# A norm weight of 1024 columns multiplied into gelu rows by GpSimd, in place of scaling 128x114 blocks as they leave PSUM, with all engine orders of the later stages written anew

## What is computed

```
h = h + _L1_ffn_ref(_layernorm(h))        # LN: D = 256
# _L1_ffn_ref:
h = einsum('btd,hd->bth', x, absmean(W_fc))      # 256 -> 1024, weights in {-1, 0, 1}
h = gelu(h, approximate=False)
h = (h - mu) * rsqrt(var + eps) * ln_w + ln_b    # over the 1024 columns
return einsum('bth,dh->btd', h, absmean(W_proj)) # 1024 -> 256
```

## Time and profile before

| | |
|---|---|
| three runs | 544.4, 544.42, 547.71 us; median 544.42 |
| the profiled execution | 544.11 us |
| its span from first to last record | 542.3 us |
| around the span | 1.8 us |
| PE / DVE / ACT / POOL busy | 92% / 70% / 52% / 36% of the span |
| bytes from HBM | 27.98 MB, the DMA engines nearly idle after 240 us |

### The profile page before, as it was taken

One profiled execution on the slowest core, in us unless ns is written; L12 is line 12 of the kernel. 1 busy time (PEld: TensorE's weight loads), 2 busy tenths in 40 slices (PEclk: granted clock), 3 DMA queues, 4 the chain that ended last, 5 costly groups with the idle time before them and its releaser, 6 DMA issues. The chain is left out here.

```text
span 542.3 us, 11847 instructions
## 1 busy us (share of the span) xinstructions
PE 498.7 (92%) x3814; PEld 418.8 (77%) x3814; DVE 380.1 (70%) x1009; ACT 280.1 (52%) x684; POOL 194.8 (36%) x257
## 2 busy tenths in 40 slices
PE   8989999999998888689999999999999998989994
PEld 8778877877786666468778888888888886877874
DVE  5554366466456767547898878778788787799884
ACT  4220321322223334547667776776776787665751
POOL 4232123132133311365464553543643601243311
PEclk9998999999999999999999999999999999999997
DMA  8934342432504100000000000000000000000000
GB/s 302 391 110 164 116 149 90 153 131 81 176 27 158 25 2 1 1 0 2 1 1 1 2 0 0 0 0 0 0 0 0 2 2 0 2 10 26 19 25 16
DMA packets 10992, 29.64 MB, mean 55 GB/s; under 512 B 2192, under 2 KB 3408, under 8 KB 10704
## 3 DMA queue, kind: packets, MB, share of 16 engines
q1 hardware_dynamic: 10960, 29.23, 16.0%
HBM read 27.98 MB, written 1.25 MB: 54 GB/s over the span
## 5 line engine op out<-in xcount | busy, mean ns | idle before, releaser
L378 POOL TENSOR_TENSOR h<-h,scaled 114x256 f32 (+1 forms) x88 | 68.5, 779 | 43.2 <-ACT scaled L695 36.5
L330 POOL TENSOR_TENSOR small<-small,half 114x1 f32<-114x1 f32 x44 | 28.6, 650 | 135.8 <-DVE small L966 135.8
L561 ACT ACTIVATE p_exp<-sc,cst 114x608 f32<-114x608 f32 x66 | 48.1, 794 | 26.8 <-DVE sc L1047 26.8
L2010 PE MATMUL bz<-ebuf 128*128 128x256 f32 x256 | 59.0, 383 | 0.0
L569 ACT ACTIVATE pt<-tb 114x456 f32<-114x456 f32 x66 | 34.4, 556 | 35.4 <-PE tb L1978 35.3
L2010 PEld LDWEIGHTS bz<-ebuf 128*128 128x128 f32 x256 | 47.9, 192 | 5.9
L1978 PE MATMUL tb<-cst,p_exp 114*114 114x114 f32 x352 | 44.1, 266 | 6.2 <-ACT pt L569 3.7
L2156 PE MATMUL score<-v,pt 114*114 114x137 f32 x352 | 48.5, 282 | 0.0
L695 ACT ACTIVATE scaled<-bank,gl 114x256 f32<-114x256 f32 x88 | 38.8, 471 | 18.1 <-PE bank L1897 10.3
L1978 PEld LDWEIGHTS tb<-cst,p_exp 114*114 114x114 f32 x352 | 35.2, 134 | 15.4 <-ACT pt L569 7.0
L2156 PEld LDWEIGHTS score<-v,pt 114*114 114x114 f32 x352 | 43.9, 178 | 1.8
(11 more groups left out here) (210 smaller groups left out, 1315.6 us busy)
## 6 DMA issues: line engine op xcount, KB each, us to landing
ebuf<-in_w_in SPq DMA_DIRECT2D x16, 512.0 KB, 4.3
ebuf<-in_w_out SPq DMA_DIRECT2D x16, 512.0 KB, 5.1
x_raw<-in_x_tiles SPq DMA_DIRECT2D x11, 342.0 KB, 3.1
out<-h SPq DMA_DIRECT2D x10, 114.0 KB
raw<-in_w_a SPq DMA_DIRECT2D x4, 256.0 KB, 4.2
ebuf<-in_fc SPq DMA_DIRECT2D x1, 1024.0 KB, 4.9
ebuf<-in_proj SPq DMA_DIRECT2D x1, 1024.0 KB, 7.0
raw<-in_w_a SPq DMA_DIRECT2D x2, 384.0 KB, 5.4
```

The lines of the kernel that those rows point to most:

```text
L378: gp.tensor_tensor(h[0:R, t, :], h[0:R, t, :], scaled[0:R, e % 4, :], ALU.add).then_inc(moe_acc, 1)
L561: act.activation(p_exp[0:R, :, b * S:(b + 1) * S], sc[0:R], ACT.Exp, bias=cst[0:R, CB + b:CB + b + 1], scale=SCALE).then_inc(exps, 1)
L2010: last = pe.matmul(bz[:, m * D:(m + 1) * D], ebuf[:, 0, c * D + m * P:c * D + (m + 1) * P], ebuf[:, 1, c * D:(c + 1) * D], start=(c == 0 a ...
```

## The change

1. `gel` becomes two buffers by tile parity; a third, `gel_w`, holds the weighted row. All lie in `ebuf`, which the expert and ternary weights have left by then; a row copy of the weight (`lnw_row`) is loaded there by one more DMA, once all four ternary steps are done.
2. POOL gets `d2_weigh`: per tile two multiplies of 114x512, after each half of gelu. `d2_turn` transposes `gel_w` and waits for each half by itself.
3. `d2_hi` and `d2_lo` no longer scale. Each evicts a half in one instruction of 128x456, in place of four of 128x114.
4. `d1_gelu(t)` now waits for the weighting and the statistics of tile t-2, no longer for the turns and statistics of t-1.
5. All order lists after the first loop, and the body of `c_step`, are different on PE, DVE, ACT and POOL. Apart from the ternary block the same instructions are in them.

```diff
-        gel = ebuf[:, 0, 0:HID]
+        gel = [ebuf[:, 0, 0:HID], ebuf[:, 1, HID:2 * HID]]
+        gel_w = ebuf[:, 0, HID:2 * HID]
+        lnw_row = ebuf[:, 1, 0:HID]
...
+            sp.wait_ge(tern, 8)
+            sp.dma_start(lnw_row[0:R], lnw).then_inc(row_w_in, 16)
...
+            def d2_weigh(t, halves):
+                if zero(t):
+                    gp.wait_ge(row_w_in, 16)
+                for q in halves:
+                    gp.wait_ge(gelu, 2 * t + q + 1)
+                    if q == 0:
+                        since(gp, gT_mm, 2 * t)
+                    cols = slice(q * 512, (q + 1) * 512)
+                    gp.tensor_tensor(gel_w[0:R, cols], gel[t % 2][0:R, cols], lnw_row[0:R, cols], ALU.mult).then_inc(weighted, 1)
...
                     if q == 0:
-                        since(act, gT_mm, 2 * t)
-                        since(act, g_stat, 4 * t - 2)
-                    act.activation(gel[0:R, q * 512:(q + 1) * 512], bk[1 + q][0:R, :], ACT.Gelu).then_inc(gelu, 1)
+                        since(act, weighted, 2 * t - 2)
+                        since(act, g_stat, 4 * t - 6)
+                    act.activation(gel[t % 2][0:R, q * 512:(q + 1) * 512], bk[1 + q][0:R, :], ACT.Gelu).then_inc(gelu, 1)
...
-                    for c in range(4):
-                        k = 4 * q + c
-                        last = act.activation(gth[:, k, :], score[:, q, c * R:(c + 1) * R], ACT.Copy, scale=lnwc[:, k:k + 1])
-                    last.then_inc(gT_hi, 1)
+                    act.activation(gth[:, 4 * q:4 * q + 4, :], score[:, q, 0:4 * R].rearrange("p (c r) -> p c r", c=4),
+                                   ACT.Copy).then_inc(gT_hi, 1)
...
-                    for c in range(4):
-                        k = 4 * q + c
-                        last = V.scalar_tensor_tensor(gtl[:, k, :], score[:, q, c * R:(c + 1) * R], lnwc[:, k:k + 1],
-                                                      gth[:, k, :].bitcast(F32), ALU.mult, ALU.subtract)
-                    last.then_inc(gT_lo, 1)
+                    V.tensor_tensor(gtl[:, 4 * q:4 * q + 4, :], score[:, q, 0:4 * R].rearrange("p (c r) -> p c r", c=4),
+                                    gth[:, 4 * q:4 * q + 4, :].bitcast(F32), ALU.subtract).then_inc(gT_lo, 1)
...
             def d2_turn(t, halves=(0, 1)):
-                pe.wait_ge(gelu, 2 * t + 2)
                 since(pe, gT_lo, 2 * t)
                 for q in halves:
+                    pe.wait_ge(weighted, 2 * t + q + 1)
...
-                        last = pe.transpose(score[:, q, c * R:(c + 1) * R], gel[0:R, k * P:(k + 1) * P], cst[0:R, CI:CI + R])
+                        last = pe.transpose(score[:, q, c * R:(c + 1) * R], gel_w[0:R, k * P:(k + 1) * P], cst[0:R, CI:CI + R])
...
             d1_fc(1, (0, 1))
+            d1_x(2)
             c3_r1(8)
+            d1_fc(2, (0,))
             c2_turn_p(10, (0,))
```

More of the change, by code:

```diff
@@ L798, in _ @@
             c1_gate(2)
             softmax_exp(0 + T, (0, 1, 2))
-            c1_scale(2, (0, 1, 2, 3))
-            c2_pt(0, (0, 1, 2))
+            c1_scale(2, (0, 1))
+            c2_pt(0, (0,))
+            c1_scale(2, (2,))
+            c2_pt(0, (1,))
+            c1_scale(2, (3,))
+            c2_pt(0, (2,))
             c1_scale(2, (4,))
             c2_pt(0, (3,))
+            c2_x(1, (0, 1))
+            c2_hi(1)
             c1_x(3)
-            c1_scale(2, (5,))
             c2_pv(0, (0, 1))
-            c2_x(1, (0, 1))
@@ new lines, in _ @@
+            c2_pv(0, (4, 5))
+            c2_mix(0)
+            softmax_exp(1 + T, (0, 1, 2))
+            c1_gate(3)
+            c2_pt(1, (0, 1, 2, 3))
+            c2_pv(1, (0,))
+            c3_att(0)
+            c2_pv(1, (1,))
+            c1_scale(3, (0, 1, 2))
+            c2_x(2, (0, 1))
+            c2_hi(2)
+            c1_scale(3, (3, 4))
+            c2_pv(1, (2, 3))
+            c2_rows(2)
+            c2_pv(1, (4, 5))
+            c2_q(2, (0,))
+            c3_x(0, (0, 1))
+            c2_q(2, (1,))
@@ L849, in _ @@
+            c2_pt(2, (2, 3))
             with act.Fori(5, T) as i:
@@ L870, in _ @@
             c1_scale(10, (7,))
[L871 removed]
+            c3_x(7, (0, 1))
+            c3_xhi(7)
+            softmax_exp(9 + T, (0, 1, 2))
             c3_rows(7)
[L873 to L877 removed]
+            c2_pt(9, (0, 1, 2, 3))
+            c3_relu(7, (0, 1, 2, 3))
             c2_x(10, (0, 1))
@@ L1578, in _ @@
+            gate(2, 2)
+            c2_aggr(1)
+            gate(2, 3)
+            c2_eps(1, (0,))
+            gate(2, 4)
+            aggr(n1, 4)
+            gate(2, 5)
+            c2_eps(1, (1,))
+            gate(2, 6)
+            gate(2, 7)
+            gate(2, 8)
+            c2_v(0, (0, 1))
+            normed2(1)
+            normed1(1)
+            ternary(0)
+            plus_eps(n1, 4)
+            c2_x(1)
+            ternary(1)
             c1_normed(4)
-            tern_th(1)
@@ L1580, in _ @@
-            normed2(1)
-            ternary(0)
-            ternary(1)
             c1_x(3)
-            normed1(1)
-            c2_x(1)
+            c2_k(1, (0, 1))
+            mix(0, 0)
             gate(3, 0)
             gate(3, 1)
+            mix(0, 1)
             gate(3, 2)
-            mix(0, 0)
-            mix(0, 1)
+            mix(0, 2)
+            c2_stats(2)
+            mix(0, 3)
+            softmax_max(1 + T)
+            mix(0, 4)
+            softmax_sub(1 + T, (0, 1))
+            mix(0, 5)
@@ L1613, in _ @@
             mix(0, 10)
+            gate(3, 6)
+            mix(0, 11)
+            mix(0, 12)
             normed2(2)
-            mix(0, 11)
+            gate(3, 7)
             normed1(2)
-            mix(0, 12)
-            ternary(2)
-            c1_x(4)
+            gate(3, 8)
             c3_sum(0)
-            c2_x(2)
             c3_stats(0)
@@ L1624, in _ @@
             plus_eps(n4, 0)
-            ternary(3)
+            c2_x(2)
+            ternary(2)
             c3_normed(0)
@@ L1660, in _ @@
             gate(10, 5)
+            d0_stats(0)
+            gate(10, 6)
+            aggr(nD, 0)
+            plus_eps(nD, 0)
+            gate(10, 7)
+            c2_x(9)
+            gate(10, 8)
             normed1(9)
-            gate(10, 6)
-            gate(10, 7)
-            gate(10, 8)
-            c2_x(9)
+            d1_norm(0)
+            d0_stats(1)
             c3_sum(7)
+            aggr(nD, 1)
             c3_stats(7)
             aggr(n4, 7)
-            d0_stats(0)
+            plus_eps(nD, 1)
@@ L1689, in _ @@
+            mix(8, 2)
+            d0_stats(2)
+            mix(8, 3)
+            aggr(nD, 2)
+            c3_normed(7)
+            mix(8, 4)
+            d1_x(0)
+            plus_eps(nD, 2)
+            softmax_max(9 + T)
+            mix(8, 5)
+            softmax_sub(9 + T, (0, 1))
+            mix(8, 6)
+            c2_v(9, (0,))
+            c3_x(7)
+            mix(8, 7)
             c2_stats(10)
-            plus_eps(nD, 1)
             c2_aggr(10)
-            mix(8, 5)
-            c2_eps(10, (0, 1))
@@ L2295, in _ @@
             a2_pv(8)
-            a1_x(10)
+            a1_qk(10)
+            c1_x(0)
             scores(9, True)
             a2_wo(8)
-            a1_qk(10)
-            c1_x(0)
             a1_v(10)
+            c1_gate(0)
             a1_turn(9, (0, 1, 2, 3))
```

983 lines of the change are left out of this document (474 added, 509 removed).

## The result

The changed kernel takes 556.4 us (median of 4 executions, 553.8 to 559.6) where the kernel before takes 544.4: a ratio of 1.022, 95% interval 1.019 to 1.025. The forecast was 547.8 us with a range up to 552.5, so the time lies above it. The profiled execution of after is the slowest of the four: 559.6 us, span 557.8, mean granted clock 0.966 (the other three 0.972 to 0.981; before 0.988 in the profiled one).

What follows compares the result with a forecast made beforehand. PE was taken as fully busy in the second loop, with time to win only in its idle time between the loops and waits in the ternary block. Sum: 544.1 - 2.5 + 2.4 + 5.8 + 1.0 - 3.0 = 547.8 us, range 540.5 to 552.5.

Steps and rivals of the forecast that it cites:

- Between the loops: Stretch between the two hardware loops: new order and less slow clock together save 2.5 us, bounds -5 and +2.
- the order: Between the loops: the new order fills PE's waits for the quotient in two first-attention tiles, -1.4 us.
- -1.1 for about two thirds of the slow stretch at 241.73: Between the loops: about two thirds of before's slow-clock stretch near 241.73 us goes, saving 1.1 us.
- The second loop: Six loop passes: c2_x waits through c2_pt on c1_gate, 0.4 us a pass, +2.4 us, bounds 0 and +6.
- The test named: Second loop: passes of 21.3 to 21.5 us, with PE idle ahead of c2_x, released by ACT, would show it right.
- The last softmax: Tile 10's exponentials: three table loads and gelus make PE wait at d1_fc(2), +5.8 us, bounds 0 and 7.
- the clock behind it: Products behind the last softmax's pause: PE's clock may fall, +1.0 us, bounds 0 to 1.6.
- The block: Ternary block: cheaper evictions leave six waits, 6.4 of 8.0 us, and no slow clock; -3.0 us, bounds +1 and -9.
- The first two: Rivals: softmax pause under 1 us and block gives 7, 537 us, chance 0.12; pause absent, block gives 3, 541, 0.15.
- the fifth: Rival, last softmax: table switches hold ACT 2.6 us for 1.28, 4 us more, 551.8 us; chance 0.04.
- A slower loop: Third rival, second loop: it costs 1 us per pass, 551.4 us; chance 0.12.
- That GpSimd sets the pace: Fourth rival, ternary block: multiply and turns form a ring, 5.2 us per tile against PE's 4.7, 553 us; chance 0.09.

Runs made afterwards that it cites:

- a_warm: Kernel before with the changed orders between the loops, plus useless PE products (fillers) in PE's waits there: 544.55 us, ratio 0.999.
- after_both: Changed kernel with fillers in PE's waits between the loops, and tile 1's gelu and d1_fc(2) moved later around the last softmax: 542.6 us, ratio 0.999.
- after_fix: Changed kernel with only tile 1's gelu and d1_fc(2) moved later around the last softmax, no fillers: 550.7 us.
- best_warm: after_both with the second loop's body put back to that of the kernel before: 540.8 us, ratio 0.992.
- best_plain: best_warm without the fillers in PE's waits between the loops: 545.7 us, ratio 1.001.
- b_gate: b_only with one swap on ACT: the gate's exponential behind the last eviction of transposed probabilities, not ahead: 545.5 us, ratio 1.002.
- b_only: Kernel before with the changed kernel's second-loop body on all four engines, all else as before: 548.9 us, ratio 1.010.
- b_two: b_only with two loop steps back at before's place, the Wf product on PE and the second relu pieces on ACT: 550.6 us.
- c_fix: Changed kernel with before's orders between the loops and loop body, and tile 1's gelu and d1_fc(2) moved later around the last softmax: 540.95 us, ratio 0.995.
- region C: The part of the change behind the second loop, with its functions; run alone, with the rest as in the kernel before: 547.6 us, ratio 1.008.
- c_nw3: c_noweight with three gelu buffers in place of two: 539.3 us.
- c_noweight: c_fix with GpSimd's 22 multiplies and the weight row's load left out, so the output lacks the norm weight: 549.6 us.

## Why the prediction was wrong, step by step

**Between the loops (forecast -2.5, bounds -5 and +2): this step failed.** Its first half, the order, was right in direction and too large: with full clock the new order stands 2.0 to 2.1 us ahead at the end of the second loop, and with the 1.6 us that the forecast itself gave to the slow stretch of before, that leaves some 0.4 to 0.5 us for the order (an estimate), where the term had 1.4. Its second half was "-1.1 for about two thirds of the slow stretch at 241.73", and this half has the wrong sign. I took the slow stretch of before as something that the new order could only shorten. It grew: after's profiled execution has a clock of 0.82 from 182 to 250 us, and the term came out at +6.3 at the product of tile 0, and at +7.3 with the 1.0 us of the next pass. A mean of 0.82 over 68 us is about 24 us at the lower level, and 0.97 is about 4; 20 us more at half speed cost up to 10 us (an estimate), and the runs at 0.82 stand 9.1 to 9.3 us behind those at 1.00. The rows of before held the warning, since waits stand close together there and the clock fell behind several of them, but none of my rivals had a longer slow stretch. The runs show the clock as the cause and not the waits themselves: the waits sum to the same 12.5 to 12.8 us, and work without use in them makes the kernel 6.6 (a_warm), 8.1 (after_both against after_fix) and 4.9 us (best_warm against best_plain) faster.

In after the clock is at its lower level soon after `c1_gate(0)` has waited 1.56 us at 205.56, and again behind the wait of 3.11 us ahead of the turns of tile 10:

```profile
208.00:212.00 4.00, 3.18 (x18) 2.15 (x20) 1.73 (x7) 0.99 (x3) 0.00 (x0) 0.50 0.00 0
...
228.00:232.00 4.00, 3.23 (x48) 2.40 (x50) 0.97 (x2) 0.39 (x1) 0.00 (x0) 0.50 0.02 4
```

A single wait of this length does not decide it: before waited 1.56 us at 218.85, between other waits, and its clock stayed at 1.00 until 242. Why the waits of after bring the clock down and those of before, with the same sum, did not is not settled.

**The second loop (forecast +2.4, bounds 0 and +6): right chain, short sum.** The chain named, `c2_x` behind `c2_pt` behind `c1_gate`, costs 0.44 us a pass by b_gate, against the 0.4 of the forecast. Another 0.27 a pass has no term in the sum; 0.71 a pass is +4.3 for six passes in b_only's trace. From the start of the product with Wf to the start of the next work of PE it is 0.90 us in b_gate and 0.68 in before, but this is not the cause either: b_two has 0.68 there again, and passes of 22.12 us. What makes the 0.27 stays open. The test named, an idle time ahead of `c2_x`, was a poor one: PE shows almost none in the passes, for hand-overs this short hide in the modelled ends of its rows.

**The last softmax (+5.8) and the clock behind it (+1.0): right.** The pause was 6.05 us, from the loads, gelus and exponentials in the order of the sum, and the clock behind it cost some 1.3; c_fix took 6.6 us away of the 6.8. All three loads took 1.28 us and started within 0.02 us of the end of the instruction ahead (465.28 + 0.60, then 465.90). The Trainium skill ("ScalarE: Activation LUTs", What ACT_TABLE_LOAD costs) adds a drain of about 1.38 us to each, which would have made the pause some 4 us longer, by an estimate from that figure; the trace shows no such time here either.

**The block (-3.0): right.** Evictions 0.552 us and rests 0.623 against 0.56 and 0.63, the multiply 1.302 against 1.272. Waits in us, by hand and then in the trace of after: `d1_fc(4)` 1.4 and 1.16, `d1_fc(6)` 1.7 and 1.47, the turns of tiles 9 and 10 0.7 each and 1.12 and 0.65, the last projection 1.7 and 1.51. `c3_x(10)` had 0.2 in place of 1.4. c_fix, which is region C without the pause, stands 3.4 us under before, and the account of after gave about 4.0; the walk had given 2.6.

**Sum.** Forecast +3.7 on the profiled execution, measured +15.5: +8.8 of the miss of 11.8 lie between the loops, 1.2 ahead of them, 2.5 from the loop to `c3_r1(8)`, and -0.65 behind. With the 1.0 us that the first pass hands back put to the order between the loops, these are +9.8 and 1.5. Against the median of after, 3.2 us of this belong to that execution's lower clock.

**The rivals.** The first two, without the pause, are refuted by its 6.05 us, and the fifth by loads of 1.28 us with no time beside them. A slower loop was right in direction at 0.7 us a pass. That GpSimd sets the pace is refuted by c_nw3: leaving every multiply out gives 1.2 us behind the loop. What the prediction did not see is that its product frees gelu's buffer early: with two gelu buffers, taking GpSimd out of the ring of the fourth rival costs 8.7 us (c_noweight). The range failed because all cases for slower were about waits, rates or the clock behind the pause, and none about the clock between the loops.

## What to carry to other kernels

Where PE already has several short waits in a row, a new order that keeps their sum can still cost more than it gives, through the clock; read the granted clock in windows of a few us, and give a reordering a case of its own for a longer slow stretch. Work without use placed in such waits is a quick test of this, and here it stayed in the fastest kernel. Before two functions with different tables are put side by side on ACT, count the loads that fall ahead of the instruction that PE waits for; and when an engine copies a tile on its way, ask what buffer that copy frees, for it may be worth more than its time. Follow a lead past the place where it arises, too: here 1.0 us of 3.0 was gone one pass later.
